# A convolution and mixture-of-experts block: raw rows with their deviation to the experts, centred weights, Newton steps, all routing ahead of the tiles

## The reference

```python
x = x + relu(conv3x3(ln_c(x), kernel, groups=8) + bias)   # x: 16 x 16 x 16 x 128 (NHWC), ln over channels, eps 1e-6
t = tokens(x)                                              # 4096 tokens of 128 channels
flat = ln_t(t)                                             # (t - mean) / sqrt(var + 1e-5)
topk_vals, topk_idx = top_k(flat @ router_w.T, 2)          # 8 experts
topk_w = softmax(topk_vals)
y_e = (silu(flat @ w_gate[e]) * (flat @ w_up[e])) @ w_down[e]   # 128 -> 256 -> 128
t = t + sum over the two chosen experts of topk_w * y_e
```

## Time and profile before

| | us |
|---|---|
| median of 3 runs | 277.31 |
| profiled execution, its own time | 278.89 |
| its span, first to last instruction | 277.2 |
| TensorE busy, matmul (1186) | 202.9 (73%) |
| VectorE busy (457 instructions) | 140.8 (51%) |
| ScalarE busy (285) | 119.0 (43%) |
| GpSimd busy (184) | 163.6 (59%) |
| mean granted TensorE clock | 0.866 of full speed |
| result scatters, L1005, 78 DMAs | 76.3, 978 ns each |
| row scatters, L992, 64 DMAs | 63.0, 984 ns each |
| product, L842, 40 | 27.1, 678 ns each |
| silu, L574, 40 | 23.5, 586 ns each |

### The profile page before, as it was taken

How to read it: one execution, slowest core, us unless ns; L and a number is a source line. 1 busy time by engine, 2 the same in 40 slices (tenths; PEclk the granted TensorE clock), 3 DMA queues, 4 the chain that set the end, 5 groups by cost and what they waited for, 6 DMA issues and landing times.

```text
span 277.2 us, 4518 instructions
## 1 busy us (share of the span) xinstructions
PE 202.9 (73%) x1186; PEld 174.3 (63%) x1186; DVE 140.8 (51%) x457; ACT 119.0 (43%) x285; POOL 163.6 (59%) x184
## 2 busy tenths in 40 slices
PE   6699576975529595739998654993999999999000
PEld 5687464864428484428887544883898789898000
DVE  3557696555241724445755322451458866555025
ACT  2369544745902353073453322342445454454100
POOL 5644388743775277725777777764356576666600
PEclk9599895999957777757999999898899999999855
DMA  7993010100133351100232232343239523361075
GB/s 235 380 381 116 0 48 30 53 29 10 48 94 82 78 115 59 48 10 31 74 87 70 68 78 78 100 134 84 61 68 303 159 72 96 99 195 43 15 237 217
DMA packets 26648, 28.99 MB, mean 105 GB/s; under 512 B 4957, under 2 KB 18409, under 8 KB 26624
## 3 DMA queue, kind: packets, MB, share of 16 engines
q1 hardware_dynamic: 21776, 20.03, 25.1%
q0 software_dynamic: 4544, 8.47, 9.1%
q10 hardware_dynamic: 304, 0.20, 0.2%
HBM read 16.93 MB, written 12.67 MB: 107 GB/s over the span
## 4 chain that ended last, share of the span: by engine, by line
PE 28%; POOL 21%; issue 13%; DVE 12%; DMA 11%; SPq 6%; ACT 6%; POOLq 1%; ACTq 0%; DVEq 0%
POOL zs L992 11%; POOL yb L1005 9%; PE ps_gu L349 7%; PE ps_y L439 5%; DMA yb<-y,zt 3%; PE ps_gu L419 3%; PE ps_gu L421 3%; PE ps_gu L420 3%; PE ps_h L429 3%; SPq L303 3%; DMA zt<-zs 3%; ACT zr L547 2%; DMA spare<-yb 2%; PE ps_z L408 2%; DVE bn L637 2%
## 5 line engine op out<-in xcount | busy, mean ns | idle before, releaser
L1005 POOL DMA_INDIRECT yb<-y,zt x78 | 76.3, 978 | 40.0 <-ACT y L583 24.6
L992 POOL DMA_INDIRECT zs<-zr,slot x64 | 63.0, 984 | 38.0 <-issue 18.3
L349 PE MATMUL ps_gu<-pad,ckw 128*128 128x256 f32 x192 | 53.7, 439 | 0.0
L349 PEld LDWEIGHTS ps_gu<-pad,ckw 128*128 128x128 f32 x192 | 41.7, 224 | 7.1
L842 DVE TENSOR_TENSOR hh<-ps_gu,sg 128x512 f32<-128x512 f32 (+1 forms) x40 | 27.1, 678 | 35.7 <-ACT sg L574 35.7
L439 PE MATMUL ps_y<-wall,hT 128*128 x312 | 41.9, 278 | 0.0
L439 PEld LDWEIGHTS ps_y<-wall,hT 128*128 128x128 f32 x312 | 38.7, 195 | 0.1
L574 ACT ACTIVATE sg<-ps_gu 128x512 f32<-128x512 f32 (+1 forms) x40 | 23.5, 586 | 33.3 <-PE ps_gu L421 33.3
L583 ACT ACTIVATE y<-ps_y,zt 128x128 f32<-128x128 f32 x78 | 24.4, 365 | 30.1 <-PE ps_y L439 30.1
L419 PE MATMUL ps_gu<-wall,z_lo 128*128 x78 | 36.4, 467 | 0.0
L408 PE MATMUL ps_z<-ident,zt 128*128 128x128 f32 x78 | 17.1, 302 | 21.2 <-DMA zt<-zs 15.2
(11 more groups left out here) (131 smaller groups left out, 225.9 us busy)
## 6 DMA issues: line engine op xcount, KB each, us to landing
zt<-zs SPq DMA_DIRECT2D x78, 65.0 KB, 2.0
spare<-yb SPq DMA_DIRECT2D x16, 256.0 KB, 4.5
xt<-x_rows SPq DMA_DIRECT2D x8, 256.0 KB, 5.3
xc<-x_cols SPq DMA_DIRECT2D x8, 256.0 KB, 6.6
spare<-gate_up_w SPq DMA_DIRECT2D x8, 256.0 KB, 6.3
out<-xt SPq DMA_DIRECT2D x8, 256.0 KB, 3.0
yb<-y,zt POOLq DMA_INDIRECT x78, 2.3
zs<-nulls SPq DMA_DIRECT2D x18, 65.0 KB, 3.3
```

The source lines that it names most:

```text
L349: last = nc.tensor.matmul(dst, ckw[:, h * BANDS + k, :], pad[n % 2][:, h * IMG:(h + 1) * IMG, below:below + PAIRS, dx:dx + WW], start=k == ...
L992: nc.gpsimd.indirect_dma_start(zs[g], bass.IndirectOffsetOnAxis(slot[:, k, n * TT + t:n * TT + t + 1], 0), zr[n % ZR][:, t, k, :], None, b ...
L1005: nc.gpsimd.indirect_dma_start(yb, bass.IndirectOffsetOnAxis(zt[:, u % RING, s, P:P + 1].bitcast(U32), 0), y[u % YB][:, s, :], None, bound ...
```

## The change

Seven edits go together.

1. The rows that are scattered are the raw sums, not normalised. `xt` and `zr` become one buffer `rows` (two copies of all chunks), with three words behind each row: id, weight, inverse deviation. The ids are written once by GpSimd. ScalarE copies each transposed chunk into `rows` twice (`copy_rows`) and writes the weight and the deviation words (`row_scalars`). `normalise_t`, `shift_t`, `write_ids`, `write_weights` and the ring go.
2. The mean is taken out of the gate and up weights: TensorE multiplies each expert's weights with a centring matrix into one PSUM bank `ps_w` (`centre_weights`), ScalarE and VectorE take the high part and the tail from there. Two experts are done in each of the iterations 3 to 6.
3. Silu takes the deviation as its scale, and the product multiplies with it; both are issued once per tile instead of once per unit.
4. The power -0.5 is computed on VectorE by three Newton steps from a bit-pattern guess (`inverse_root`, ten instructions), for chunks 4 to 7 of x and for all batches of t but the first.
5. The last batch is routed before the first tile is transposed; the second set's table is made in unit 0 and 1.
6. `pass_on` and one more matmul carry the count of earlier batches into the rank, so that `slots` has one step less.
7. The router's weights come transposed and are centred by a matmul; the first power runs once early without a use; `pads` of chunks from 2 on are both on ScalarE; the loads of the gate and up weights move behind those of x.

```diff
+        def inverse_root(v, dst):
+            nc.vector.tensor_scalar(r.bitcast(I32), v.bitcast(I32), -0.5, MAGIC, ALU.mult, ALU.add)
+            for k in range(3):
+                nc.vector.scalar_tensor_tensor(square[:, 0:c], r, -0.5, r, ALU.mult, ALU.mult)
+                nc.vector.tensor_tensor(scaled[:, 0:c], square[:, 0:c], v, ALU.mult)
+                nc.vector.scalar_tensor_tensor(to, scaled[:, 0:c], 1.5, r, ALU.add, ALU.mult)
...
+            def centre_weights(e):                                   # TensorE
+                pe.wait_ge(ew_loaded[e], 16)
+                if e >= 1:
+                    pe.wait_ge(w_lo_ready, e)
+                nc.tensor.matmul(ps_w, centre[:], ew[:, e], start=True, stop=True).then_inc(w_ready_ps, 1)
...
             for n in range(CHUNKS):                                  # TensorE
                 conv(n, 0)
                 if n >= 1:
-                    rows_and_logits(n - 1)
+                    logits(n - 1)
+                    transpose_t(n - 1)
                 if n + 1 < CHUNKS:
                     transpose_x(n + 1)
+                e = 2 * (n - CENTRE_STEP)                            # CENTRE_STEP is 3
+                if 0 <= e < E:
+                    centre_weights(e)
                 conv(n, 1)
-                for b, (c0, c1) in enumerate(BATCHES):
-                    if n == c1:
-                        rank(b)
+                if n - 1 in BATCH_AT:                                # last chunk of a batch -> batch
+                    rank(BATCH_AT[n - 1])
+                if 0 <= e < E:
+                    centre_weights(e + 1)
                 if n == SET_CHUNKS[0][1] + 1:
                     table(0)
-            rows_and_logits(CHUNKS - 1)
+            logits(CHUNKS - 1)
+            transpose_t(CHUNKS - 1)
+            rank(LAST)
...
             for n in range(CHUNKS + 1):                              # ScalarE
+                e = 2 * (n - CENTRE_STEP)
                 if n >= 1:
                     conv_relu(n - 1, 1)
+                if 0 <= e - 2 < E:
+                    weight_heads(e - 1)
+                if n - 2 in BATCH_AT:
+                    row_scalars(BATCH_AT[n - 2])
-                if 1 <= n and n + 1 < CHUNKS:
+                if 1 <= n < CHUNKS - 1:
                     normalise_x(n + 1)
                 if n < CHUNKS:
                     conv_relu(n, 0)
-                if n + 1 < CHUNKS:
-                    pad_evens(n + 1)
                 if n >= 1:
                     copy_rows(n - 1)
-                if n < 2:
-                    for e in range(4 * n, 4 * n + 4):
-                        weight_heads(e)
-                for b, (c0, c1) in enumerate(BATCHES[:-1]):
-                    if n == c1:
-                        pair_weight(b)
-                        normalise_t(c0)
-                    if n == c1 + 1 and c1 == c0 + 2:
-                        normalise_t(c0 + 1)
+                if n + 1 < CHUNKS:
+                    pads(n + 1)
+                if 0 <= e < E:
+                    weight_heads(e)
+            row_scalars(LAST)
...
             for n in range(CHUNKS):                                  # VectorE
+                e = 2 * (n - CENTRE_STEP)
+                if 0 <= e < E:
+                    weight_tails(e)
+                residual(n)
+                if n - 1 in BATCH_AT:
+                    slots(BATCH_AT[n - 1])
+                    if not closes(BATCH_AT[n - 1]):
+                        pass_on(BATCH_AT[n - 1])
+                if n in (2, 4):
+                    stats_x(n + 2)
+                    stats_x(n + 3)
+                    variance_x(n // 2 + 2)
+                    shift_x(n // 2 + 2)
                 if n == SET_CHUNKS[0][1] + 2:
                     table_row(0)
+                stats_t(n)
+                if n == SET_CHUNKS[0][1]:
                     table(0)
+                if n in BATCH_AT:
+                    deviation_t(BATCH_AT[n])
+                if 0 <= e < E:
+                    weight_tails(e + 1)
+                if n in BATCH_AT:
+                    top_two(BATCH_AT[n])
+                    scale_gap(BATCH_AT[n])
+            slots(LAST)
             z_tails(0)
             for u in range(UNITS + 2):
                 if u + 1 < UNITS:
                     z_tails(u + 1)
                 if u < UNITS:
                     gated(u)
                 if u == 0:
-                    top_two(LAST)
-                    scale_gap(LAST)
-                    shift_t(LAST)
+                    table(1)
+                if u == 1:
+                    table_row(1)
                 if 1 <= u <= UNITS:
                     h_cols(u - 1)
...
+                for s in range(COUNT[u]):                            # silu, ScalarE
+                    last = nc.scalar.activation(sg[u % 2][:, s, :], ps_gu[u % 2][:, s * N:s * N + H], ACT.Silu,
+                                                scale=zt[:, u % RING, s, RSTD:RSTD + 1])
...
+                for s in range(COUNT[u]):                            # gated, VectorE
+                    last = nc.vector.scalar_tensor_tensor(
+                        hh[u % 2][:, s, :], ps_gu[u % 2][:, s * N + H:(s + 1) * N], zt[:, u % RING, s, RSTD:RSTD + 1],
+                        sg[u % 2][:, s, :], ALU.mult, ALU.mult)
...
+            pool.wait_ge(ids_ready, 2 * len(SETS))                   # GpSimd
+            alone = CHUNKS - 2
+            for n in range(alone):
+                dispatch(n, 0, 2 * TT)
             u = 0
-            for n in range(*BATCHES[LAST]):
+            for n in range(alone, CHUNKS):
                 for i in range(0, 2 * TT, 2):
                     dispatch(n, i, i + 2)
                     combine_rows(u)
                     u += 1
```

More of the change, by code:

```diff
@@ L109, in metaformer_moe @@
         relu = [sb(f"relu{b}", [P, N]) for b in range(2)]
-        zr = [sb(f"zr{b}", [P, TT, 2, ROW]) for b in range(ZR)]
         bn1, bn2 = sb("bn1", [P, TT, 6]), sb("bn2", [P, TT, 6])
@@ L277, in load_units @@
                 held = sum(COUNT[first:last])
-                _, rows = nc.values_load_multi_w_load_instructions(
+                _, starts = nc.values_load_multi_w_load_instructions(
                     tab[g][0:1, TILES[g] + i:TILES[g] + i + held], engines=[mybir.EngineType.SP],
@@ L285, in load_units @@
                     for s in range(COUNT[u]):
-                        sp.dma_start(zt[:, u % RING, s, :], zs[g][bass.ds(rows[2 * (u - first) + s], P), :]
+                        sp.dma_start(zt[:, u % RING, s, :], zs[g][bass.ds(starts[2 * (u - first) + s], P), :]
                                      ).then_inc(zt_loaded[u % RING], 16)
@@ L353, in conv, with transpose_t, logits @@
                 last.then_inc(conv_ready, 1)
-            def rows_and_logits(n):
-                b = BATCH_OF[n]
-                pe.wait_ge(t_ready, n + 1)
-                if n >= 2:
-                    pe.wait_ge(t_copied, n - 1)
-                for t in range(TT):
-                    last = nc.tensor.transpose(ps_t[n % 2][:, t * P:(t + 1) * P], xc[:, n, t * P:(t + 1) * P], ident[:])
-                last.then_inc(t_rows_ready, 1)
+            def transpose_t(n):
+                pe.wait_ge(t_ready, n + 1)
+                if n >= 1:
+                    pe.wait_ge(t_copied, 2 * n)
+                for t in range(TT):
+                    last = nc.tensor.transpose(ps_t[:, t * P:(t + 1) * P], xc[:, n, t * P:(t + 1) * P], ident[:])
+                last.then_inc(t_rows_ready, 1)
+            def logits(n):
+                b = BATCH_OF[n]
                 if n == BATCHES[b][0] and b >= 2:
@@ L375, in rank @@
                 pe.wait_ge(mask_ready, b + 1)
+                pe.wait_ge(passed_ready, len(SETS) + b - SET_OF_BATCH[b])
                 dst = ranks_of(b)
                 nc.tensor.matmul(dst, upper[:], mask[:, BT - held:BT + 1, :], start=True, stop=False)
+                nc.tensor.matmul(dst, ones[:], passed[:, b:b + 1, :].broadcast_to([P, held + 1, E]),
+                                 start=False, stop=False)
                 for t in range(held):
@@ L445, in _ @@
             keep_warm(12)
-            pe.wait_ge(rw_step, 3)
-            nc.tensor.transpose(ps_h[:, 0:E], rw_c[:], ident[0:E, 0:E]).then_inc(rwT_ready, 1)
-            keep_warm(4)
+            pe.wait_ge(rw_loaded, 16)
+            pe.wait_ge(centre_ready, 2)
+            nc.tensor.matmul(ps_h[:, 0:E], centre[:], rwT[:], start=True, stop=True).then_inc(rwT_ready, 1)
+            keep_warm(8)
             transpose_x(0)
@@ L734, in top_two @@
                     dve.wait_ge(rank_ready, b)
+                    dve.wait_ge(held_summed, sum(not closes(a) for a in range(b)))
                 nc.vector.tensor_tensor(mask[:, BT - c:BT, :], oh[:, 0, 0:c], oh[:, 1, 0:c], ALU.add
@@ L773, in write_weights @@
-            def write_weights(b):
-                c0, c1 = BATCHES[b]
-                dve.wait_ge(th_ready, b + 1)
-                for n in range(c0, c1):
```

(18 more changed lines are left out.)

438 lines of the change are left out of this document (182 added, 256 removed).

## The result

The changed kernel takes 292.03 us (median of 4 runs, 288.57 to 293.64), the kernel before on the same chip 277.35: ratio 1.047 (95% interval 1.037 to 1.058). It is 14.7 us slower; forecast were 6.8, with a range of 274 to 291.5, so the median of the four lies 0.5 us above the range. The profiled execution, 293.64 us for a span of 291.9, is the slowest of the four and counts as a slow one; the other three (288.57 to 292.56 us) give the ratio, and 1.047 times 277.31 is 290.3 us, inside the range. A second measurement gave 293.17 against 278.22: 1.050 (1.040 to 1.060).

What follows compares the result with a forecast made beforehand. No engine bounds throughout; time is the first result store's start plus a tail of 148.3 us. Store at 135.5 for 128.98 (6.5 late) and 0.3 in the tail shift the 277.31 median by 6.8 to 284.1 us; range 274 to 291.5.

Steps and rivals of the forecast that it cites:

- cause (1): Routing stage: with one bank ps_w, even centring and the half convolution behind it wait for the odd weight tail behind the deviation.
- cause (2): Routing stage: statistics and Newton steps of chunks 4 to 7 stand behind slots, ScalarE's normalise waits; 5.6 and 5.2 us.
- cause (3): Routing stage: VectorE computes the deviation, 2.35 us, ahead of the top two, 3.0 us.
- The Newton steps: VectorE's inverse root: ten steps of 0.205 us, 2.1 us a call; nothing added for contention with GpSimd.
- half clock: TensorE after waits over 4 us: centring matmul 1.7 us for 0.85, half convolution 4.2 for 2.65.
- the sum to chunk 2: From slots of chunk 1 to slots of chunks 2 and 3: 29.7 us, ending at 70.1.
- The tail: First result store to the end: 148.3 us before, left as it is but for 0.3 us exposed at the end.
- the split: Silu and product per tile: each about 0.15 us more per unit, covered by TensorE; uncovered 8 us.
- (a): Rival: the convolution and routing ring keeps its old pace, first store at 114.9, 14.1 us early, 263.2 us; chance 0.10.
- (b): Rival: Newton steps held by GpSimd, 7 us, or silu and product per tile uncovered, 8 us: 292 us; chance 0.12.
- (c): Rival: TensorE keeps full clock behind three waits and in gate and up: 8.5 us less, 275.6 us; chance 0.13.
- (d): Rival: early gains and later losses cancel, leaving 277.3 us; chance 0.03.

Runs made afterwards that it cites:

- c_after: The changed kernel itself, unaltered, measured a second time beside other experiments: 293.17 us, ratio 1.050 to the kernel before.
- e6_merged: Changed kernel with silu and product issued once per unit again, the scale by the deviation left out of both: 289.53 us, ratio 1.038 to the kernel before.
- e11_top_stats: Changed kernel with odd weight tail and top two ahead of t's statistics and deviation, x's statistics and Newton steps one iteration earlier: 272.33 us, ratio 0.979.
- e14_spread: e11_top_stats with the last batch's deviation and its scalars in unit 0, the second set's table in units 1 and 2: 263.75 us, ratio 0.951.

## Why the prediction was right in kind and short in size

*Slower, by waits that the orders make.* Right, and shown: moving cause (1) alone takes 4 points of the ratio, cause (2) alone 2.6, cause (3) another 2.7 on top of (1), and (1) and (3) together turn the change into a gain (0.981). The Newton steps are no refuted rival beside it: with the orders left as they are, taking them out brings the ratio to 1.000 too. The time is lost where both meet, steps that stand in a queue ahead of what others wait for. The size came out at twice the forecast, 14.7 us for 6.8.

*The forecast's milestones.* First scatter 30.1: measured 30.23. Slots of chunk 1 at 40.4: they end at 42.25. Chunk 2 scattered from 71: 74.47. Chunk 4 from 108.0 (107.0 plus 0.95): 111.69. First store 135.5: 140.42. Tail 148.5: 151.5. TensorE transposed z at 126.86, well behind the 117 that would have spoken against the forecast, and in the stretch from 221 to 227 us a unit took 2.95 us, as before. The span came out 7.9 us over the forecast's 284.0, in these terms: 1.85 before chunk 1, 1.6 to chunk 2, 0.3 to chunk 4, 1.2 to the first store, 3.0 in the tail. The 0.3 and the 1.2 us were not followed up.

*The clock* was the mechanism with the wrong rule. I priced the half clock only "where TensorE has waited over 4 us", and that step failed. Before chunk 1, where the forecast had no sum but a place read off the old trace, the half convolution at 28.24 followed a wait of 1.86 us and took 4.53 for 2.65; that is the 1.85 us. In the sum to chunk 2, the transposes and centring(0) at 49.43 and 50.34 followed a wait of 2.42 us and took 1.11 and 1.91 us for the 0.45 and 0.85 of the forecast, as much as the 1.6 us that are missing there. c_after shows that the same instruction can go either way: there chunk 1 scattered 3.2 us earlier, at 39.66, but chunk 2 only 1.05 us earlier, since two half convolutions in between took 4.36 and 4.90 us for the 2.96 and 4.20 of the first execution. The kernel before had both kinds already, 5.09 us behind a wait of 4.12 and 2.84 behind one of 3.61:

```profile
64.36 0.21 PE L377 MATMUL ps_y<-mask,upper 128*128 128x72 bf16 x1 [3.61 <-DVE mask L735]
```

*The tail* was the second term that came out wrong: "exposed once at the end, 0.3 us", and it grew by 3.3 us over that of before. TensorE is nearly full in the stretch that I had looked at, 19.84 of 20 us in the row below for 20.00 in the earlier trace rows, so most of the cover for the split is there. Nor is the split shown to be the cause: e6_merged, without it, has a tail of 150.0 us, 1.8 over that of before. About half of the growth stands at one place, where the tiles of the second set begin: TensorE waits 5.97 us for a tile's load, where it waited 4.54, and GpSimd waits 7.64 us for result rows, where it waited 6.03 (e6_merged: 7.71). The forecast had no term for these loads. Why they come later, and the other half, stay open.

The rows of the kernel before, and the changed kernel's of TensorE (GpSimd's is the last row of the first list):

```profile
193.05 0.69 PE L408 MATMUL ps_z<-ident,zt 128*128 128x128 f32 x2 [4.54 <-DMA zt<-zs]
...
197.72 0.97 POOL L1005 DMA_INDIRECT yb<-y,zt  x1 [6.03 <-ACT y L583]
```

```profile
203.55 0.69 PE L432 MATMUL ps_z<-ident,zt 128*128 128x128 f32 x2 [5.97 <-DMA zt<-zs]
```

The stretch of the changed kernel that answers to the second row:

```profile
220.00:240.00 20.00, 19.84 (x129) 17.20 (x128) 17.24 (x36) 11.35 (x33) 12.97 (x14) 1.00 0.60 185
```

*Newton.* 0.205 us a step was right (pitch 0.20), and 2.1 us a call. So were the five calls in the sum; a sixth, for chunk 1, lay ahead of them. That next to nothing is added for GpSimd was right too: the ten steps from 45.39 to 47.50 ran beside indirect DMAs, eight at 0.17 us and two at 0.23, and of all 36 Newton steps beside a GpSimd instruction in this trace three took over 0.20 us, the longest 0.28. The Trainium skill, "GPSIMD Engine Reference", section Specifications, would have them contend; this trace shows 0.2 us of it over 36 steps. (The table's pace of 0.18 us in the forecast was a mean: one step of that stretch took 0.37.) What I did not see is that steps on the ring also cost clock elsewhere: 15.5 us together, for 10.8 of their own.

*The signs to look for.* GpSimd idle 51 to 71 and 91 to 108: it was 52.8 to 74.5 and 94.6 to 111.7. TensorE idle over 4 us before centring: 4.59, 4.58, 4.60. ScalarE waiting for the shift twice: 5.63 and 4.58.

*Rivals.* (a), the ring keeps its pace, 263.2 us with the first store at 114.9: false for this kernel, but it is what the reordered one does (first store 114.33 in e11_top_stats and 111.02 in e14_spread, the latter at 263.75 us). (b) gave 292 us, which is the measured time, by a mechanism that did not happen: GpSimd added 0.2 us to the Newton steps and not 7, and without the split (e6_merged) the kernel gained 3.6 us at most and not 8. A number that fits is no proof of its reason. (c), no half clock: false in all three places. (d): false.

*Not tried:* what the 5.31 us stall of the old ring was worth by itself.

## What to carry to other kernels

In a ring of engines that hand work to one another, order each engine's queue by who waits for the result: what another engine waits for (the mask, the weight tail that frees a bank) goes ahead of what only a queue with slack needs (the deviation, used at the scatter). Here that order alone was worth 27 us (ratio 0.951 for 1.050), with the same work. Price a wait on TensorE with the slower matmuls behind it, also for waits of 2 us: taking nine of ten small steps out of each call in another engine's queue gave back 1.4 times their own time (15.5 us for 10.8). The Trainium skill, "TensorE: Matmul & The Clock Gate", section "HAM oscillation — how this bites in real kernels", tells of a kernel whose short bursts each started at the lower clock after a wait for DMA; the traces agree, with waits for VectorE in place of DMA (granted clock 0.57 to 0.62 in the stretches behind three waits of 4.6 us).

## What the runs showed of the hardware

- The length of the wait just before does not tell the clock behind it. In the changed kernel a wait of 1.86 us was followed by a half convolution of 4.53 us, and one of 1.85 at the same place of c_after by one of 2.84; in e11_top_stats one of 1.57 us by 4.02, and one of 2.85 us by 2.76, full speed:

```profile
53.94 1.57 PE L392 MATMUL ps_gu<-spare,centre 128*128 128x512 f32 x2 [1.57 <-DVE wall L855]
55.30 4.02 PE L362 MATMUL ps_gu<-pad,ckw 128*128 128x256 f32 x12
...
83.33 1.10 PE L392 MATMUL ps_gu<-spare,centre 128*128 128x512 f32 x2 [2.85 <-DVE wall L855]
84.26 2.76 PE L362 MATMUL ps_gu<-pad,ckw 128*128 128x256 f32 x12
```

- The same program's runs spread: the changed kernel from 288.57 to 293.64 us, e11_top_stats from 266.35 to 273.6. That this comes from the clock is likely, since two traces of the changed kernel differ by it, but it is not shown run by run.
- Chips can differ far more than that: the kernel before took 277.35, 278.22, 277.57 and 278.21 us in four comparisons and 315.98 in the fifth, on a chip of its own; the traces of the four kernels that ran beside it have idle time that the profile ties to no wait. Why is open; it is a reason to run the kernel before beside every experiment.
